# A cross-attention kernel's first context segment: from fp32 matmuls to three fp32r passes over split halves

## The chip, the cores and the metric

One Trainium2 chip, one of its cores. The metric is the device time of one execution in microseconds (us); the median of several runs is given. The engines of the core are PE (TensorE, the matrix engine), DVE (VectorE), ACT (ScalarE), POOL (GpSimd) and SP (SyncE, which issues the DMAs here). PEld stands for the weight loads of PE.

## What is computed

For 128 batches of 128 positions, x has 320 channels and the context 512. The context's 128 tokens fall into four segments: 77, 4, 4 and 43 tokens, each with weights of its own for keys and values. Attention runs with 20 heads of 16 channels; the four results are added.

```python
q = _heads(hidden_states @ to_q_w)
h_txt = _sdpa(q, _heads(ehs_txt @ to_k_w), _heads(ehs_txt @ to_v_w))
h_obj = _sdpa(q, _heads(ehs_obj @ to_k_object_w), _heads(ehs_obj @ to_v_object_w))
h_oth = _sdpa(q, _heads(ehs_oth @ to_k_others_w), _heads(ehs_oth @ to_v_others_w))
h_ip = _sdpa(q, _heads(ehs_ip @ to_k_ip_w), _heads(ehs_ip @ to_v_ip_w))
out = _merge(h_txt) + _merge(h_obj) + _merge(h_oth) + _merge(h_ip)
out = out @ to_out_w + to_out_b + hidden_states
```

## The kernel before

Four batches make a **group**, and there are 32 groups. The main loop has one **turn** g per group, and a turn has ten **slots**; each engine has its own program of slots (`groups`, line 271), and semaphores tie them together.

Attention works in **octets**: eight (batch, head) pairs, ten octets a group. In slot n:

- PE makes the scores of octet n + 2 (`scores`), transposes the probabilities of octet n - 2 in two quarters of four heads (`transpose_p`, line 913) and, in some slots, multiplies with the values (`values`, line 926) and with the output weights (`project`, line 936). The results of these three go through two PSUM banks, the ring, which ACT or DVE empties in turn.
- DVE takes the maxima of octet n + 1 and subtracts them (`reduce_max`, `shift`), then sums the exponentials of octet n and inverts the sums (`sum_up`, line 718, `invert`, line 729).
- ACT makes the exponentials of octet n (line 580) and copies PE's results.
- POOL multiplies the probabilities of octet n - 1 by the inverses (`scale`, lines 491 and 494). PE's transposition of an octet waits for it.

Between these, PE projects for the groups ahead. The **jobs** of a turn stand in `SEQ`: ("q", 0..2) make the queries of group g + 2, ("kv", 0..2) keys (and the head of the values) of group g + 2, ("kv", 3..4) the values of group g + 1, ("v", 0..3) transpose them. Two PSUM banks alternate between jobs; a job waits until the job two before it has left its bank. `PIECES` puts them into slots, by hand: a "kv" job comes in two halves.

```python
PIECES = [(0, 0, ("kv", 3), 0), (0, 1, ("kv", 3), 1), (1, 0, ("kv", 4), 0), (2, 0, ("kv", 4), 1), (3, 0, ("q", 0), None),
          (3, 1, ("v", 0), None), (4, 1, ("q", 1), None), (5, 0, ("v", 1), None), (5, 1, ("q", 2), None),
          (6, 0, ("v", 2), None), (6, 1, ("kv", 0), 0), (7, 0, ("kv", 0), 1), (7, 1, ("v", 3), None),
          (8, 0, ("kv", 1), 0), (8, 1, ("kv", 1), 1), (9, 0, ("kv", 2), 0), (9, 1, ("kv", 2), 1)]
```

A "kv" job (`work`, line 821) multiplies 128 rows of weights with the group's context `c_in`: half 0 is the first segment (77 tokens of four batches, 308 columns), half 1 the last segment (43 tokens, 172 columns). Both are fp32, four chunks of 512 channels; the trace shows each fp32 matmul as two records, so eight records a half (line 837). The two small segments were projected for all groups at the start (`small_job`, line 804) and are added by one matmul with the identity (line 847).

A query job is done in fp32r instead: x is split into a high half (ACT, `x_high`, line 574) and a low half (POOL, `x_low`, line 480), the weights as well, and three passes high·high, high·low and low·high are summed in PSUM (line 863). The projection at the end does the same with 320 columns (line 936).

A query or key job is then split into three bf16 parts: ACT writes the first (`evacuate`, line 562) once the job is done, DVE subtracts it from PSUM (`subtract_part`, line 708), which frees the bank, and POOL makes the other two (`split`, lines 472 and 475). SP stores them to scratch and loads them back as stacks (`store_parts`, `load_pair`). A stack pair holds two batches of a group.

POOL's program of a slot is, in this order: `scale` of octet n - 1, the splits of the jobs that ended two slots ago, `oT_low` (line 523) in slots 0, 2, 5 and 7, `x_low` in slots 9, 0 and 1. So slot 5 splits ("q", 0), slot 6 ("q", 1), slot 7 ("q", 2), slot 9 ("kv", 0). ACT's program of a slot is the exponential, evacuations, copies of the ring, evacuations, the spreading of values (line 613), `x_high`.

Context: `load_c(g + 2)` is issued in turn g once PE has finished ("kv", 4), in slot 2.

Before the loop, groups 0 and 1 are projected in `EARLY_JOBS`, and all weights are loaded and split. SP's order there is lines 376 to 412. `pads_made` counts memsets on DVE (lines 743 to 749) for which PE's first matmul waits. The projections of the small tokens for groups 2 to 31 lie in `pT` and go to scratch in one store of 2400 KB (line 406).

Of the kernel before, what the change touches and what calls it, by code (L numbers as in the profile page):

```python
# [5 lines left out]
B, S, T = 128, 128, 128  # L6
C, CA = 320, 512
H = 20
# [31 lines left out]
N_CONSTS = 5  # L40
N_PADS = 6
# [100 lines left out]
def xattn_kernel(nc: bass.Bass, x, xT, cT, cT_small, wq, wk, wv, wko, wvo, wkt, wvt, wki, wvi, wo, bo, out):  # L142
# [13 lines left out]
    with ExitStack() as stack:  # L156
# [12 lines left out]
        c_in = sb("c_in", [P, CK, NB, T])  # L169
        c_small = sb("c_small", [P, len(SMALL), CK, NB * B])  # L170
        x_res = sb("x_res", [P, 2, C])
# [3 lines left out]
        w_q2 = sb("w_q2", [P, 3, CT])  # L175
        w_kv = sb("w_kv", [P, len(LARGE), CK, 2 * C])
        w_q = [sb(f"w_q{i}", [P, 3, 3 * P], fp32r) for i in range(2)]
        w_o = [sb(f"w_o{i}", [P, 3, C], fp32r) for i in range(2)]
# [28 lines left out]
        wo_raw = y_all[:, 0:3 * C].rearrange("p (k c) -> p k c", k=3)  # L207
        v_flat = v_pad[:, :, :, :].rearrange("p b h w -> p (b h w)")

        s_ps = [banks(f"s_ps{i}", 2) for i in range(2)]  # L210
# [15 lines left out]
        x_lo_made = sem("x_lo_made")  # L226
        w_hi_made = sem("w_hi_made")
        w_lo_made = sem("w_lo_made")
        small_filled = sem("small_filled")
# [70 lines left out]

        W_FIRST = [(wq_raw[:, 0:2, :], w_q[0][:, 0:2, 0:C]), (wq_raw[P - CT:P, 2, :], w_q[0][P - CT:P, 2, 0:C]),
                   (wq_raw[0:CT, 2, :], w_q[1][0:CT, 2, 0:C])]
        W_SECOND = [(wq_raw[:, 0:2, :], w_q[0][:, 0:2, 0:C], w_q[1][:, 0:2, 0:C]),
                    (wq_raw[0:CT, 2, :], w_q[1][0:CT, 2, 0:C], w_q[0][0:CT, 2, 0:C])]

        @block.sync
        def _(sp):
# [63 lines left out]
            def load_w(dst, s, which, loaded):  # L371
                i = SMALL.index(s) if s in SMALL else LARGE.index(s)
                sp.dma_start(dst[:, i, :, which * C:(which + 1) * C],
                             seg_w[s][which].rearrange("(k p) c -> p k c", p=P)).then_inc(loaded, 16)
# [7 lines left out]
            for i in range(len(SMALL)):  # L382
                sp.dma_start(c_small[:, i, :, :], cT_small[i]).then_inc(few_loaded[i], 16)
                for which in range(2):
                    load_w(w_small, SMALL[i], which, few_loaded[i])
            load_c(0)
            for which in range(2):
                for s in LARGE:
                    load_w(w_kv, s, which, w_kv_loaded)
            load_x(1)  # L390
# [3 lines left out]
            sp.dma_start(wo_raw[0:CT, 2, :], wo[2 * P:C, :]).then_inc(w_o_loaded, 16)  # L394
            sp.wait_ge(pads_made, N_PADS)
            sp.dma_start(wo_raw[CT:CT + 1, 2, :], bo.rearrange("(a c) -> a c", a=1)).then_inc(w_o_loaded, 16)
# [54 lines left out]
        def _(pool):  # L451

            for t in w_q:
                pool.memset(t[:, :, C:3 * P].bitcast(fp32), 0.0).then_inc(consts_made, 1)
            pool.memset(zero[:, :], 0.0).then_inc(consts_made, 1)
# [20 lines left out]

            def x_low(g, k):
# [48 lines left out]
            def slot(g, n):  # L526

                if live(g * NO + n - 1, G * NO):
                    scale(g if n else g - 1, (n - 1) % NO)
                for at in range(2):  # L530
                    for turn, job in ended(g, n - 2, at):
                        if job in SPLITS:
                            split(turn + 2, SPLITS.index(job))
                if n in VALUES_AT and live(g * NB + VALUES_AT[n], B):
                    oT_low(g * NB + VALUES_AT[n])
                for k, (at, ahead) in enumerate(XLO_AT):
                    if at == n and live(g + ahead, G) and not (isinstance(g, int) and g + ahead < 3):
                        x_low(g + ahead, k)
# [4 lines left out]
        def _(act):  # L543
            def evacuate(turn, job):
# [12 lines left out]
                else:  # L557
# [57 lines left out]

            act.wait_ge(consts_made, 2)
            act.wait_ge(w_q_loaded, 16 * N_W_Q)
# [5 lines left out]
            act.wait_ge(consts_made, N_CONSTS)  # L623
            act.wait_ge(pads_made, N_PADS)
            for turn, job in EARLY_JOBS:
                evacuate(turn, job)
                if (turn, job) == (-2, ("q", 2)):
                    for k in range(CX):
                        x_high(1, k)
            spread(0, 0)  # L630
            spread(0, 1)
# [5 lines left out]
            def slot(g, n):  # L637
# [16 lines left out]
                if n in SPREAD_AT:  # L654
                    ahead, i = SPREAD_AT[n]
                    if live(g + ahead, G):
                        spread(g + ahead, i)
                for k, (at, ahead) in enumerate(XHI_AT):
                    if at == n and live(g + ahead, G) and not (isinstance(g, int) and g + ahead < 3):
# [5 lines left out]
        def _(dve):  # L665
# [81 lines left out]
            dve.memset(v_flat, 0.0).then_inc(pads_made, 1)  # L747
            dve.wait_ge(pads_made, N_PADS - 1)
            dve.memset(oT_raw[CT:CT + 1, 2, :], 1.0).then_inc(pads_made, 1)
# [8 lines left out]
            for turn, job in EARLY_JOBS:  # L758
# [3 lines left out]
                if (turn, job) == (-1, ("kv", 3)):  # L762
                    for n in range(len(SMALL) * MK, N_SMALL):
                        copy_small(n)
                if (turn, job) == EARLY_JOBS[-1]:
                    reduce_max(0, 0)
# [27 lines left out]
        def _(pe):  # L794

            def small_job(n):
# [6 lines left out]
                for k in range(CK):  # L803
                    last = pe.matmul(ring_ps[n % 2][:, :], w_small[:, i, k, m * P:(m + 1) * P], c_small[:, i, k, :],  # L804
                                     start=(k == 0), stop=(k == CK - 1))
# [15 lines left out]
            def work(turn, job, half=None):  # L821
# [56 lines left out]
            def scores(g, o):  # L878

                n = g * NO + o  # L880
                if o % NR == 0:
                    pe.wait_ge(stack_loaded[o // NR], (g + 1) * 16 * 2)
# [56 lines left out]

            pe.wait_ge(w_lo_made, len(W_SECOND))  # L940
            pe.wait_ge(pads_made, N_PADS)
            pe.wait_ge(ident_made, 1)
# [74 lines left out]
```

## Time and profile before

| | |
|---|---|
| median of 3 runs | 1705.54 us (1705.48 to 1706.51) |
| the profiled execution's own time | 1707.59 us |
| its span, first to last instruction | 1705.5 us |
| mean granted clock of TensorE | 0.992 of 2.4 GHz |
| PE, DVE, ACT, POOL busy | 95%, 88%, 63%, 79% |
| DMA | 366 MB, 215 GB/s |

Busy shares are of the span. A PE that is busy by its records is not PE at its peak, since matmuls overlap; where the pace of matmuls matters, the distance from start to start is read. Idle time in a row is that of the engine just before the instruction, with what released it.

### The profile page before, as it was taken

The numbers are of one execution on the slowest core, as the hardware profiler recorded it, in microseconds if no ns is written. First come the engines' busy times: TensorE is split into PE (matmuls) and PEld (weight loads), VectorE is DVE, ScalarE is ACT, GpSimd is POOL, SyncE is SP. The second block draws the span as 40 slices with busy tenths as digits, with TensorE's granted clock in tenths as the row PEclk, the third lists the DMA queues.
The fourth block names the chain that finished last, engine by engine and source line by source line (L and its number), as shares of the span: only waits on it lengthen the run. The fifth ranks groups of instructions, "written<-read, shape, count | busy, mean of one in ns | idle before, by whom it ended". The sixth has DMA issues, their size and how long they took to land.

```text
span 1705.5 us, 49968 instructions
## 1 busy us (share of the span) xinstructions
PE 1623.6 (95%) x15632; PEld 1377.6 (81%) x15632; DVE 1498.3 (88%) x3537; ACT 1076.2 (63%) x1989; POOL 1342.3 (79%) x1581
## 2 busy tenths in 40 slices
PE   6959999999999999999999999999999999999976
PEld 3658888888888888888888888888888888888865
DVE  4249999999999999999999999999999999999996
ACT  1126666666666666676666667666666666666664
POOL 4248888888888888888888888888888888888765
PEclk9979999999999999999999999999999999999999
DMA  8579889888988988898898889889888988988851
GB/s 303 140 208 234 205 228 239 203 227 217 241 206 227 237 205 227 217 238 209 227 235 205 227 218 238 208 230 232 207 226 219 238 208 231 230 207 229 207 124 32
DMA packets 423236, 366.24 MB, mean 215 GB/s; under 512 B 19041, under 2 KB 394274, under 8 KB 418850
## 3 DMA queue, kind: packets, MB, share of 16 engines
q1 hardware_dynamic: 423202, 365.80, 84.7%
q8 instruction: 20, 0.33, 0.1%
q14 instruction: 14, 0.11, 0.0%
HBM read 216.38 MB, written 149.34 MB: 214 GB/s over the span
## 4 chain that ended last, share of the span: by engine, by line
PE 71%; DVE 17%; issue 7%; POOL 2%; SPq 1%; DMA 1%; DVEq 1%; ACT 0%; POOLq 0%
PE job_ps L837 24%; PE ring_ps L913 13%; PE ring_ps L926 7%; PE ring_ps L936 7%; PE s_ps L886 6%; PE job_ps L863 5%; DVE l_seg L718 5%; DVE probs L691 5%; DVE m_seg L675 3%; PE job_ps L856 2%; PE ring_ps L804 2%; PE job_ps L866 2%; DVE rest L708 1%; POOL probs L491 1%; PE job_ps L874 1%
## 5 line engine op out<-in xcount | busy, mean ns | idle before, releaser
L491 POOL TENSOR_TENSOR probs<-probs,rl 128x616 f32<-128x616 f32 (+1 forms) x640 | 630.1, 1007 | 237.2 <-DVE rl L729 236.8
L837 PE MATMUL job_ps<-c_in,w_kv 128*128 128x172 f32 (+1 forms) x2560 | 575.5, 368 | 22.4 <-DVE rest L708 22.4
L592 ACT ACTIVATE pT<-ring_ps 128x512 f32<-128x512 f32 x640 | 378.6, 599 | 313.1 <-PE ring_ps L913 309.1
L837 PEld LDWEIGHTS job_ps<-c_in,w_kv 128*128 128x128 f32 x2560 | 421.4, 190 | 101.0 <-DVE rest L708 30.0
L718 DVE TENSOR_REDUCE l_seg<-probs 128x8 f32<-128x616 f32 (+1 forms) x640 | 385.4, 644 | 23.0 <-ACT probs L580 23.0
L913 PE MATMUL ring_ps<-ident,probs 128*128 128x128 f32 x2560 | 389.9, 277 | 10.1 <-DVE y_all L740 8.5
L691 DVE TENSOR_TENSOR probs<-s_ps,m_seg 128x616 f32<-128x616 f32 (+1 forms) x640 | 387.8, 648 | 0.0
L675 DVE TENSOR_REDUCE m_seg<-s_ps 128x8 f32<-128x616 f32 (+1 forms) x640 | 371.6, 623 | 3.5 <-issue 0.2
L580 ACT ACTIVATE probs<-probs 128x1024 f32<-128x1024 f32 x320 | 337.6, 1055 | 33.2 <-DVE probs L695 33.1
L913 PEld LDWEIGHTS ring_ps<-ident,probs 128*128 128x128 f32 x2560 | 290.0, 143 | 66.7 <-issue 25.1
L472 POOL TENSOR_TENSOR parts<-rest,zero 128x512 bf16<-128x512 f32 (+1 forms) x192 | 186.2, 970 | 50.7 <-DVE rest L708 50.7
L475 POOL TENSOR_TENSOR parts<-rest,parts 128x512 bf16<-128x512 f32 (+1 forms) x192 | 207.2, 1079 | 15.0
L708 DVE TENSOR_TENSOR rest<-job_ps,parts 128x512 f32<-128x512 f32 (+1 forms) x192 | 122.9, 640 | 109.4 <-ACT parts L562 109.3
L886 PE MATMUL s_ps<-k_all,q_all 128*128 128x128 bf16 x2560 | 197.6, 220 | 19.6 <-DVE probs L695 19.5
L936 PE MATMUL ring_ps<-w_o,oT 128*128 128x320 f32 x1152 | 202.1, 320 | 8.1 <-ACT pT L592 5.7
L886 PEld LDWEIGHTS s_ps<-k_all,q_all 128*128 128x128 bf16 x2560 | 163.8, 101 | 52.9 <-issue 24.7
L926 PE MATMUL ring_ps<-pT,v_pad 128*32 128x128 f32 x5120 | 194.7, 277 | 0.0
L936 PEld LDWEIGHTS ring_ps<-w_o,oT 128*128 128x128 f32 x1152 | 171.1, 189 | 15.1 <-ACT pT L592 12.5
L926 PEld LDWEIGHTS ring_ps<-pT,v_pad 128*32 128x32 f32 x5120 | 159.8, 110 | 14.0 <-issue 0.8
L599 ACT ACTIVATE oT_raw<-ring_ps 128x256 f32<-128x256 f32 x128 | 49.5, 387 | 172.3 <-PE ring_ps L926 171.6
L523 POOL TENSOR_TENSOR oT<-oT_raw,oT 128x384 fp32r<-128x384 f32 x128 | 128.4, 1003 | 27.8 <-ACT oT L605 27.8
L562 ACT ACTIVATE parts<-job_ps 128x512 bf16<-128x512 f32 (+1 forms) x192 | 106.6, 555 | 55.5 <-PE job_ps L847 37.0
(54 smaller groups left out, 1598.2 us busy)
## 6 DMA issues: line engine op xcount, KB each, us to landing
q_all<-q_scratch SPq DMA_DIRECT2D x64, 960.0 KB, 8.1
k_all<-k_scratch SPq DMA_DIRECT2D x64, 960.0 KB, 12.3
c_in<-in_cT SPq DMA_DIRECT2D x32, 1024.0 KB, 5.1
x_raw<-in_xT SPq DMA_DIRECT2D x32, 768.0 KB, 4.8
q_scratch<-parts SPq DMA_DIRECT2D x64, 384.0 KB, 3.0
k_scratch<-parts SPq DMA_DIRECT2D x64, 384.0 KB, 5.2
x_res<-in_x SPq DMA_DIRECT2D x128, 160.0 KB, 3.8
out<-y_all SPq DMA_DIRECT2D x128, 160.0 KB, 3.5
```

The source lines that it names most:

```text
L475: pool.tensor_tensor(dst[:, 2, :], src, dst[:, 1, :], ALU.subtract).then_inc(part3_made, 1)
L491: pool.tensor_tensor(pr[:, :, a:e], pr[:, :, a:e], r[:, :, s:s + 1].broadcast_to((P, OH, e - a)), ALU.mult)
L580: act.activation(pr, pr, ACT.Exp, scale=SCALE).then_inc(exp_done, 1)
L592: act.activation(pT[:, h:h + QH, :], ring_ps[i][:, :].rearrange("p (h s) -> p h s", h=QH), ACT.Copy)\
L675: dve.tensor_reduce(m_seg[:, o % 2, :, k:k + 1], sc[:, :, a:e], axis=AX.X, op=ALU.max)\
L691: dve.tensor_tensor(pr[:, :, a:e], sc[:, :, a:e], m_seg[:, o % 2, :, k:k + 1].broadcast_to((P, OH, e - a)), ALU.subtract)
L718: dve.tensor_reduce(l_seg[:, o % 2, :, s:s + 1], pr[:, :, a:e], axis=AX.X, op=ALU.add)
L837: last = pe.matmul(dst[:, :, a:e], w_kv[:, l, k, i * P:(i + 1) * P], c_in[:, k, :, a:e], start=(k == 0), stop=(k == CK - 1))
L886: last = pe.matmul(s_ps[o % 2][:, i * T:(i + 1) * T], q_st[s // 2][:, h, s % 2, :], k_st[s // 2][:, h, s % 2, :], start=True, stop=True)
L913: last = pe.transpose(ring_ps[i][:, k * S:(k + 1) * S], probs[:, (o % NR) * OH + q * QH + k, :], ident[:, :])
L926: last = pe.matmul(ring_ps[i][a * VW:(a + 1) * VW, k * S:(k + 1) * S], v_pad[:, s, h, :], pT[:, (s % 2) * H + h, :], start=(e == 0), stop= ...
L936: last = pe.matmul(ring_ps[i][:, 0:C], oT[a][:, k, :], w_o[c][:, k, :], start=(k == 0 and (a, c) == (0, 0)), stop=(k == 2 and (a, c) == (1 ...
```

## The change

The first segment's projection becomes three fp32r passes, as the queries' already are. Its width is rounded up to an even `W0` = 78 tokens, 312 columns for four batches (the column too many is overwritten by the matmul of the small tokens). The context's high halves `c0[0]` are made by ACT and the low halves `c0[1]` by POOL, in two pieces of two chunks each, 128x624: on ACT both at the end of slot 5, on POOL one each in slots 5 and 6, behind what these slots do already. The halves of a "kv" job are exchanged: half 0 is now the last segment (fp32, 172 columns), half 1 the first segment in 12 passes and the small tokens. The first of these passes for ("kv", 0) waits for both low halves. Group 0 keeps the fp32 matmuls.

The weights' halves `w0` take the room of `c_small` and part of `w_q`; so the small tokens' inputs are loaded into the second half of the stacks' memory, the raw weights into that of the padded values, and their memsets come later (`stacks_padded`, the last of `pads_made`). The unused zero columns of `w_q` fall away with their memsets on POOL. The 2400 KB store of the small tokens is issued before `load_c(1)`, no longer after three stores of group 1's queries, and the load of the second stack pair waits for the small jobs.

```diff
+W0 = SEGS[0][1] + SEGS[0][1] % 2
+CHI_AT, CLO_AT = [5, 5], [5, 6]
...
+        c_small = [t[:, H * 2 * S:NPAIR * H * 2 * S].bitcast(fp32)[:, 0:CK * NB * B].rearrange("p (k n) -> p k n", k=CK)
+                   for t in (q_all, k_all)]
...
             load_small(1)
+            sp.dma_start(small_scr[2:G].rearrange("g p n -> p g n"),
+                         small_all[:, 2:G, :, :, :].rearrange("p g m b t -> p g (m b t)")).then_inc(small_rest_stored, 16)
             load_c(1)
             for n in range(3):
                 store_parts(1, n)
-            sp.dma_start(small_scr[2:G].rearrange("g p n -> p g n"),
-                         small_all[:, 2:G, :, :, :].rearrange("p g m b t -> p g (m b t)")).then_inc(small_rest_stored, 16)
+            sp.wait_ge(small_filled, N_SMALL)
             load_pair(0, 0, 1)
...
+            def c_low(g, i):
+
+                pool.wait_ge(c_hi_made, (g - 1) * 2 + i + 1)
+                a = 2 * i
+                pool.tensor_tensor(c0[1][:, a:a + 2, :, :].rearrange("p k b t -> p (k b) t"),
+                                   c_in[:, a:a + 2, :, 0:W0].rearrange("p k b t -> p (k b) t"),
+                                   c0[0][:, a:a + 2, :, :].bitcast(fp32).rearrange("p k b t -> p (k b) t"), ALU.subtract)\
+                    .then_inc(c_lo_made, 1)
...
+            for m in range(MKV):
+                pool.wait_ge(w0_hi_made, m + 1)
+                pool.tensor_tensor(w0[1][:, :, m * P:(m + 1) * P], w0_raw[:, :, m * P:(m + 1) * P],
+                                   w0[0][:, :, m * P:(m + 1) * P].bitcast(fp32), ALU.subtract).then_inc(w0_lo_made, 1)
             for n in range(NSP):
+                if n == 3:
+                    for i in range(2):
+                        c_low(1, i)
                 split(1, n)
...
                     oT_low(g * NB + VALUES_AT[n])
+                for i in range(2):
+                    if CLO_AT[i] == n and live(g + 2, G):
+                        c_low(g + 2, i)
...
+            def c_high(g, i):
+
+                act.wait_ge(c_loaded, (g + 1) * 16)
+                act.activation(c0[0][:, 2 * i:2 * i + 2, :, :], c_in[:, 2 * i:2 * i + 2, :, 0:W0], ACT.Copy).then_inc(c_hi_made, 1)
...
                         spread(g + ahead, i)
+                for i in range(2):
+                    if CHI_AT[i] == n and live(g + 2, G):
+                        c_high(g + 2, i)
...
-            dve.memset(k_all[KS:P, :].bitcast(fp32), 0.0).then_inc(pads_made, 1)
-            dve.memset(q_all[KS:P, :].bitcast(fp32), 0.0).then_inc(pads_made, 1)
+            dve.memset(k_all[KS:P, 0:H * 2 * S].bitcast(fp32), 0.0).then_inc(pads_made, 1)
+            dve.memset(q_all[KS:P, 0:H * 2 * S].bitcast(fp32), 0.0).then_inc(pads_made, 1)
...
-                    for l, s in enumerate(LARGE):
-                        if half in (None, l):
-                            a, e = SEGS[s]
-                            for k in range(CK):
-                                last = pe.matmul(dst[:, :, a:e], w_kv[:, l, k, i * P:(i + 1) * P], c_in[:, k, :, a:e],
-                                                 start=(k == 0), stop=(k == CK - 1))
+                    if half in (None, 0):
+                        a, e = SEGS[3]
+                        for k in range(CK):
+                            pe.matmul(dst[:, :, a:e], w3[:, k, m], c_in[:, k, :, a:e], start=(k == 0), stop=(k == CK - 1))
...
+                    if half in (None, 1) and not whole_first:
+                        if i == 0:
+                            pe.wait_ge(c_lo_made, g * 2)
+                            if first:
+                                pe.wait_ge(w0_lo_made, MKV)
+                        for k in range(CK):
+                            for a, c in ((0, 0), (0, 1), (1, 0)):
+                                pe.matmul(dst[:, :, 0:W0], w0[a][:, k, m], c0[c][:, k, :, :],
+                                          start=(k == 0 and (a, c) == (0, 0)), stop=(k == CK - 1 and (a, c) == (1, 0)))
```

## Rows read from the trace of the kernel before

**Rows 1.** The page: busy time by engine; the chain that ended last, by engine.

```profile
PE 1623.6 (95%) x15632; PEld 1377.6 (81%) x15632; DVE 1498.3 (88%) x3537; ACT 1076.2 (63%) x1989; POOL 1342.3 (79%) x1581
...
PE 71%; DVE 17%; issue 7%; POOL 2%; SPq 1%; DMA 1%; DVEq 1%; ACT 0%; POOLq 0%
```

**Rows 2.** Timeline of PE: start us, us, instructions, [idle before <- releaser].

```profile
500.27 2.34 PE L837 MATMUL job_ps<-c_in,w_kv 128*128 128x308 f32 x8 [0.70 <-DVE rest L708]
...
823.85 0.63 PE L913 MATMUL ring_ps<-ident,probs 128*128 128x128 f32 x4
...
845.01 1.33 PE L837 MATMUL job_ps<-c_in,w_kv 128*128 128x172 f32 x8
...
846.32 0.64 PE L913 MATMUL ring_ps<-ident,probs 128*128 128x128 f32 x4
...
848.87 2.34 PE L837 MATMUL job_ps<-c_in,w_kv 128*128 128x308 f32 x8 [0.70 <-DVE rest L708]
```

**Rows 3.** Timeline of DVE, 800 to 852 us.

```profile
805.15 0.69 DVE L708 TENSOR_TENSOR rest<-job_ps,parts 128x512 f32<-128x512 f32 x1 [1.44 <-ACT parts L562]
...
826.59 1.21 DVE L718 TENSOR_REDUCE l_seg<-probs 128x8 f32<-128x616 f32 x2 [0.26 <-ACT probs L580]
...
848.14 0.68 DVE L708 TENSOR_TENSOR rest<-job_ps,parts 128x512 f32<-128x512 f32 x1
```

**Rows 4.** Chain that ended last, 800 to 840 us: start us, us.

```profile
801.85 1.33 PE ring_ps L936 x9
...
805.38 2.08 PE job_ps L837 x8
...
825.38 1.39 PE job_ps L863 x6
```

**Rows 5.** Timeline of ACT, slot 6's exponential.

```profile
836.89 1.07 ACT L580 ACTIVATE probs<-probs 128x1024 f32<-128x1024 f32 x1
```

**Rows 6.** Groups by line and shape: count | busy us, mean ns | idle before.

```profile
L480 POOL TENSOR_TENSOR x_lo<-x_raw,x_hi 128x512 fp32r<-128x512 f32 x96 | 122.3, 1276 | 20.3 <-ACT x_hi L574 20.2
...
L574 ACT ACTIVATE x_hi<-x_raw 128x512 fp32r<-128x512 f32 x96 | 56.1, 622 | 23.5 <-DMA x_raw<-in_xT 23.5
...
L501 POOL TENSOR_TENSOR w_q<-parts,w_q 128x640 fp32r<-128x640 f32 x1 | 1.5, 1544 | 5.9 <-ACT w_q L619 5.9
```

**Rows 7.** Timeline of POOL, slots 5 and 6 of a turn.

```profile
833.49 1.97 POOL L491 TENSOR_TENSOR probs<-probs,rl 128x616 f32<-128x616 f32 x2 [2.85 <-DVE rl L729]
...
835.68 1.04 POOL L472 TENSOR_TENSOR parts<-rest,zero 128x512 bf16<-128x512 f32 x1
...
837.91 1.01 POOL L523 TENSOR_TENSOR oT<-oT_raw,oT 128x384 fp32r<-128x384 f32 x1
838.88 1.98 POOL L491 TENSOR_TENSOR probs<-probs,rl 128x616 f32<-128x616 f32 x2
```

**Rows 8.** Timeline of SP's DMA issues, start-up.

```profile
90.09 0.59 SPq L406 DMA_DIRECT2D small_scratch<-pT  x1
...
106.17 0.43 SPq L330 DMA_DIRECT2D x_raw<-in_xT  x1
```

**Rows 9.** Timeline of ACT, start-up.

```profile
113.99 1.67 ACT L574 ACTIVATE x_hi<-x_raw 128x512 fp32r<-128x512 f32 x3 [14.25 <-DMA x_raw<-in_xT]
```

**Rows 10.** DMA issues: count, size, median us from issue to landing.

```profile
small_scratch<-pT SPq DMA_DIRECT2D x1, 2400.0 KB, 10.5
```

**Rows 11.** Busy time by stretch: length, engines, then PEclk, DMA share, GB/s.

```profile
75.00:90.00 15.00, 11.31 (x62) 8.30 (x62) 2.50 (x4) 4.20 (x9) 6.00 (x7) 1.00 0.63 201
100.00:105.00 5.00, 4.69 (x21) 3.76 (x22) 2.77 (x8) 0.00 (x0) 1.25 (x2) 0.68 1.16 221
```

**Rows 12.** Waits: engine, line <- releaser: us in total, times, longest us.

```profile
POOL parts L472 <- DVE rest L708: 50.7, 11, 20.3
```

**Rows 13.** Timeline of PE, start-up.

```profile
100.31 1.03 PE L886 MATMUL s_ps<-k_all,q_all 128*128 128x128 bf16 x8 [2.66 <-DVE probs L695]
101.14 4.47 PE L837 MATMUL job_ps<-c_in,w_kv 128*128 128x308 f32 x16
```

More of the change, by code:

```diff
@@ L39 @@
 N_SMALL = len(SMALL) * MKV
-N_CONSTS = 5
+N_CONSTS = 3
 N_PADS = 6
@@ L169, in xattn_kernel @@
         c_in = sb("c_in", [P, CK, NB, T])
-        c_small = sb("c_small", [P, len(SMALL), CK, NB * B])
+        c0 = [sb(f"c0_{i}", [P, CK, NB, W0], fp32r) for i in range(2)]
         x_res = sb("x_res", [P, 2, C])
@@ L175, in xattn_kernel @@
         w_q2 = sb("w_q2", [P, 3, CT])
-        w_kv = sb("w_kv", [P, len(LARGE), CK, 2 * C])
-        w_q = [sb(f"w_q{i}", [P, 3, 3 * P], fp32r) for i in range(2)]
+        w3 = sb("w3", [P, CK, 2 * C])
+        w0 = [sb(f"w0_{i}", [P, CK, 2 * C], fp32r) for i in range(2)]
+        w_q = [sb(f"w_q{i}", [P, 3, 2 * P], fp32r) for i in range(2)]
         w_o = [sb(f"w_o{i}", [P, 3, C], fp32r) for i in range(2)]
@@ L227, in xattn_kernel @@
         w_hi_made = sem("w_hi_made")
+        w0_hi_made = sem("w0_hi_made")
+        w0_lo_made = sem("w0_lo_made")
+        c_hi_made = sem("c_hi_made")
+        c_lo_made = sem("c_lo_made")
+        stacks_padded = sem("stacks_padded")
         w_lo_made = sem("w_lo_made")
@@ L382, in _ @@
             for i in range(len(SMALL)):
-                sp.dma_start(c_small[:, i, :, :], cT_small[i]).then_inc(few_loaded[i], 16)
+                sp.dma_start(c_small[i], cT_small[i]).then_inc(few_loaded[i], 16)
                 for which in range(2):
-                    load_w(w_small, SMALL[i], which, few_loaded[i])
+                    load_w(w_small[:, i, :, :], SMALL[i], which, few_loaded[i])
             load_c(0)
@@ L388, in _ @@
                 for s in LARGE:
-                    load_w(w_kv, s, which, w_kv_loaded)
+                    load_w(w0_raw if s == 0 else w3, s, which, w_kv_loaded)
             load_x(1)
@@ L623, in _ @@
             act.wait_ge(consts_made, N_CONSTS)
-            act.wait_ge(pads_made, N_PADS)
+            act.wait_ge(pads_made, N_PADS - 1)
             for turn, job in EARLY_JOBS:
+                if (turn, job) == (-1, ("kv", 0)):
+                    for i in range(2):
+                        c_high(1, i)
                 evacuate(turn, job)
@@ L629, in _ @@
                         x_high(1, k)
+                if (turn, job) == (-2, ("kv", 2)):
+                    act.wait_ge(w_kv_loaded, 16 * 4)
+                    for m in range(MKV):
+                        act.activation(w0[0][:, :, m * P:(m + 1) * P], w0_raw[:, :, m * P:(m + 1) * P], ACT.Copy)\
+                           .then_inc(w0_hi_made, 1)
+            act.wait_ge(pads_made, N_PADS)
             spread(0, 0)
@@ L657, in slot @@
                         spread(g + ahead, i)
+                for i in range(2):
+                    if CHI_AT[i] == n and live(g + 2, G):
+                        c_high(g + 2, i)
                 for k, (at, ahead) in enumerate(XHI_AT):
@@ L764, in _ @@
                         copy_small(n)
+                if (turn, job) == (-1, ("kv", 3)):
+                    for t in (k_all, q_all):
+                        dve.memset(t[KS:P, H * 2 * S:NPAIR * H * 2 * S].bitcast(fp32), 0.0).then_inc(stacks_padded, 1)
+                if (turn, job) == (-1, ("q", 1)):
+                    dve.wait_ge(w0_lo_made, MKV)
+                    dve.wait_ge(job_filled, job_count(-1, ("kv", MKV - 1)))
+                    dve.memset(v_flat, 0.0).then_inc(pads_made, 1)
                 if (turn, job) == EARLY_JOBS[-1]:
@@ L803, in small_job @@
                 for k in range(CK):
-                    last = pe.matmul(ring_ps[n % 2][:, :], w_small[:, i, k, m * P:(m + 1) * P], c_small[:, i, k, :],
+                    last = pe.matmul(ring_ps[n % 2][:, :], w_small[:, i, k, m * P:(m + 1) * P], c_small[i][:, k, :],
                                      start=(k == 0), stop=(k == CK - 1))
@@ L832, in work @@
                         pe.wait_ge(c_loaded, (g + 1) * 16)
-                    for l, s in enumerate(LARGE):
-                        if half in (None, l):
-                            a, e = SEGS[s]
-                            for k in range(CK):
-                                last = pe.matmul(dst[:, :, a:e], w_kv[:, l, k, i * P:(i + 1) * P], c_in[:, k, :, a:e],
-                                                 start=(k == 0), stop=(k == CK - 1))
+                    m = slice(i * P, (i + 1) * P)
+                    whole_first = isinstance(g, int) and g == 0
+                    if half in (None, 0):
+                        a, e = SEGS[3]
+                        for k in range(CK):
+                            pe.matmul(dst[:, :, a:e], w3[:, k, m], c_in[:, k, :, a:e], start=(k == 0), stop=(k == CK - 1))
+                    if half in (None, 1) and whole_first:
+                        a, e = SEGS[0]
+                        for k in range(CK):
+                            pe.matmul(dst[:, :, a:e], w0_raw[:, k, m], c_in[:, k, :, a:e], start=(k == 0),
+                                      stop=(k == CK - 1))
+                    if half in (None, 1) and not whole_first:
[3 more added lines that the diff above has]
+                                pe.wait_ge(w0_lo_made, MKV)
+                        for k in range(CK):
+                            for a, c in ((0, 0), (0, 1), (1, 0)):
+                                pe.matmul(dst[:, :, 0:W0], w0[a][:, k, m], c0[c][:, k, :, :],
+                                          start=(k == 0 and (a, c) == (0, 0)), stop=(k == CK - 1 and (a, c) == (1, 0)))
                     if half in (None, 1):
@@ L880, in scores @@
                 n = g * NO + o
+                if isinstance(g, int) and (g, o) == (0, NR):
+                    pe.wait_ge(stacks_padded, 2)
                 if o % NR == 0:
```

22 lines of the change are left out of this document (9 added, 13 removed).

## The prediction

> **What bounds the kernel now.** The page comes first: PE is busy 95% of the span, DVE 88%, and the chain that ended last is PE for 71% and DVE for 17% [rows 1]. So PE sets most of the time, but not all of it; the question is where in a turn of the loop DVE takes over. The PE timeline shows the period: the first half of ("kv", 1) starts at 500.27 and, seven turns later, at 848.87, so a turn is 49.80 us, and both times PE has idled 0.70 us for DVE's subtraction [rows 2]. It is the only idle time of PE in a steady turn.
>
> The DVE timeline says why [rows 3]. At 826.59 DVE begins a sum after an idle 0.26 us for ACT's exponential; from there to the subtraction of ("kv", 0) at 848.14 it has no idle time. So a turn has two legs. **Leg A**, PE-bound: from ("kv", 1) at 799.07 (848.87 less a turn) through ("kv", 2), 3 and 4 to the transposition at 823.85 [rows 2], then ACT, then DVE's sum at 826.59 [rows 3]: 27.52 us. DVE itself idled 1.44 us in it at 805.15 and 0.26 at its end, so it could end 1.70 us sooner if PE did. **Leg B**, DVE-bound: 826.59 to 848.87, 22.28 us.
>
> **What the passes save.** The first segment's half job is 8 records of 2.08 us in the chain; the fp32r projection does 9 passes over 320 columns in 1.33, 0.148 each, and 6 over 512 take 1.39, 0.232 each [rows 4]. Between them a column costs 0.44 ns, so 312 columns (four sequences of 78) take 0.1445 and 12 passes 1.73 us. The new shape is not in the trace: 0.145 and 0.232 are its ends, and I take the first, since 320 columns are nearest. A job saves 0.35 us. Leg A holds four such jobs: **-1.38 us**, less than DVE's 1.70, so all of it counts.
>
> **What the halves cost, in leg B.** A group gets two ACT copies and two POOL subtractions of 128x624.
> ACT: 512 elements take 0.622 us and 1024 take 1.07 [rows 5, 6], so 624 are about 0.72. They come at the end of slot 5, where the next thing on ACT is the exponential at 836.89 [rows 5], with the evacuation of ("q", 2) and the copy of a transposition behind it. All are pushed back by about 1.2 us; PE then waits for its ring about 1 us before ("kv", 0). That wait is covered: PE waits for POOL right after.
> POOL: the subtraction of 512 elements takes 1.276, of 640 1.544 [rows 6]; 624 are 1.51, and 1.47 from start to start. POOL waits 2.85 us for DVE, begins slot 5's scaling at 833.49, then the split of ("q", 0) at 835.68, the low half of oT at 837.91, the scaling at 838.88 [rows 7] and the split of ("q", 1). The new order, in the same frame: first low half 838.88 to 840.35, scaling (2.19, as from 833.49 to 835.68) to 842.54, split of ("q", 1) (2.23, from 835.68 to 837.91) to 844.77, second low half to 846.28.
> PE: the second half of ("kv", 0) began at 845.01 and the job ended at 846.32 [rows 2]. Now it is this half which needs both low halves. PE is there at about 845.1 (0.92 sooner, since the halves of a job are exchanged: 2.08 less 1.16, the 172 columns' share of it; and 1.0 later by the ring), and waits until 846.33. Then 1.73, 0.15 for the small tokens (1.31 from 845.01 to 846.32, less 1.16) and 0.1 added for the start after a wait: 848.31. **Behind the waiting matmuls** on PE stand the transposition at 846.32 [rows 2] and everything after it; ACT copies that transposition before it evacuates the job, and DVE subtracts 1.82 us after the job's end (846.32 to 848.14, [rows 2, 3]): now 850.13, with DVE waiting 1.99 us. PE's next ("kv", 1) needs that bank: 850.86 for 848.87. Leg B is **+1.99 us**.
> DVE's reciprocal needs POOL's scaling of two octets before; that one (842.54 at the latest) is still in time. The rest of POOL's 3 us falls into its waits for DVE.
>
> **A turn: -1.38 + 1.99 = +0.6 us; 30 turns have ("kv", 0): +18 us.** The drain after the last projections is DVE's and keeps its length.
>
> **The start-up.** SP issues the 2400 KB store of the small tokens at 90.09, ahead of the stack loads; x of group 2 is issued at 106.17 [rows 8], and ACT waits 14.25 us for it, until 113.99, before the first exponential can go [rows 9]. The change issues that store before the load of c(1), some 15 us sooner. It takes 10.5 us from issue to landing [rows 10]; the DMA engines were busy 0.63 of 75 to 90 us [rows 11], so 5.5 us of work fit there. Bounds 0 and 10.5; I take **-7 us**, near the 5.5, as the rest pushes c(1) and the stores of q back. c(1) then lands some 5 us late and the jobs of group 1 wait for its halves, which still ends before x of group 2 has landed. The halves of the first segment's weights (5 ACT copies, 5 POOL subtractions of about 1.3) lie in POOL's wait of up to 20.3 us [rows 12], the memsets put off in DVE's waits of the same stretch, the shorter memsets and query weights before the first matmul are ahead of this same landing: all nothing. Were the weights' cover gone, it would be 6.4 us once.
>
> **Sum.** The profiled execution took 1707.6 (span 1705.5 and 2.1 around it): 1707.6 + 18 - 7 = 1718.6. The median of the runs is 2.1 below the profiled time, so **1716.5**. Some 0.2% (3.4 us) is what a measurement can tell from no change.
>
> **Rivals.**
> - *The halves come in time (faster).* Place: PE's wait before the second half of ("kv", 0). If POOL had the second low half ready by about 844.4, leg B would not grow: 30 x -1.38 - 7 = -48, 1657. It decides at 1.9 us less on POOL than I count; break-even is a growth of leg B of 1.38 + 7/30 = 1.6. For it: POOL idles 2.85 us just before [rows 7]; if DVE's reciprocal came sooner, all would move. Against: that start is DVE's, and DVE is full. Chance 0.24, mostly of part of it, down to 1690.
> - *The two nearly cancel*, leg B growing by 1.5 to 1.7: 1702 to 1709. 0.15.
> - *The clock falls too.* After an idle 2.66 us at 100.31 [rows 13], PE's granted clock averaged 0.68 over 100 to 105 [rows 11], a mix of 1.2 and 2.4 GHz; the 16 records of a job at 101.14 took 4.47 [rows 13], against 2.08 + 1.16 in a turn. The new waits (1.2 and 0.9 us) are shorter than that one, though longer than 0.70. If each turn lost 1.1 us so: +33, about 1750. 0.04.
> - *The passes are no faster* (the change does not do what it says): at 0.232 each, 12 take 2.78. Leg A +2.8, leg B 1.99 + 1.05: 5.8 a turn, +175, about 1873. Against: nine projections at 0.148 [rows 4]. 0.02.
>
> The Trainium skill, in "TensorE: Matmul & The Clock Gate", section "The mechanism", says that a weight load overlaps with a running matmul only where the row groups differ; with its section "LDWEIGHTS" (128 columns at 1.2 GHz) a pass would by estimate be 107 + 130 = 237 ns and the sum that of the last rival. The projection's 148 ns [rows 4] contradict it, and the measurement decides.
>
> **How the numbers follow.** The forecast (slower) has 0.55. Its own range is 1703 to 1730: 0.02 us a pass is 0.24 us a job, so some 1 us in a turn, but so large an error is unlikely; 0.1 us on each POOL subtraction is 6 us in all, the start-up 5. For 8 in 10 I go from 1694 to 1738: it takes in the cancelling case and the mild part of the first rival. Faster 0.24, within 0.2% 0.15, slower 0.55 + 0.04 + 0.02 = 0.61.
>
> **What would show it.** Right: a PE idle of over 1 us each turn before the second half of ("kv", 0), released by POOL; a turn of about 50.4 us; x of group 2 landing 7 us sooner. Wrong: that half starting without a wait, a turn under 49.5 us; POOL's subtraction well off 1.5 us; passes off 0.145; ACT, through the delayed copies, appearing as PE's releaser instead of POOL.

## The result, and the profile after

**1708.68 us** in the median of 17 runs (1707.29 to 1711.47), beside 1706.26 (1705.26 to 1708.14) for the kernel before in as many runs on the same chips: a ratio of **1.0016**, 95% interval 1.0008 to 1.0023 (the two medians by themselves differ by 2.4 us, 0.14%). The change is a loss of 0.16%, smaller than the 0.6% forecast, and within the 0.2% that the prediction called the same. The profiled execution took 1708.46, of which 1706.7 are its span, 1.2 more than before.

The page of the kernel after, the lines that answer to [rows 1]:

```profile
PE 1582.3 (93%) x16252; PEld 1421.6 (83%) x16252; DVE 1497.4 (88%) x3539; ACT 1116.5 (65%) x2056; POOL 1431.4 (84%) x1646
...
POOL 60%; issue 25%; PE 7%; DVE 4%; POOLq 1%; DMA 1%; SPq 1%; ACT 1%; ACTq 0%
```

PE does 41 us less work than before, and the time does not follow. POOL does 89 us more, and the chain that ended last, which was PE for 71%, is now POOL for 60%. The question of the view is which POOL instruction PE waits for, and where in a turn. PE's timeline from slot 5 of one turn into slot 8, with ("kv", 1) of the next turn, the answer to [rows 2] (start us, us, instructions, idle before and its releaser):

```profile
835.80 1.58 PE L1003 MATMUL ring_ps<-w_o,oT 128*128 128x320 f32 x9 [0.87 <-ACT pT L626]
...
840.36 0.66 PE L980 MATMUL ring_ps<-ident,probs 128*128 128x128 f32 x4
841.91 2.00 PE L902 MATMUL job_ps<-c,w 128*128 128x312 f32 x12 [0.90 <-POOL c L491]
...
846.43 1.43 PE L889 MATMUL job_ps<-c_in,w 128*128 128x172 f32 x8 [0.68 <-DVE rest L753]
...
849.46 1.88 PE L902 MATMUL job_ps<-c,w 128*128 128x312 f32 x12
851.18 0.30 PE L912 MATMUL job_ps<-small,ident 128*128 128x32 f32 x2
...
896.56 1.43 PE L889 MATMUL job_ps<-c_in,w 128*128 128x172 f32 x8 [0.68 <-DVE rest L753]
```

A turn had one idle stretch of PE, 0.70 for DVE; now it has three: 0.87 for ACT at the ring, 0.90 for POOL's second low half ahead of the passes of ("kv", 0), and 0.68 for DVE ahead of ("kv", 1). ("kv", 1) starts at 846.43, and at 896.56 in the next turn: 50.13 us (50.14 in the mean of 29 turns), where it was 49.80. The twelve passes with no wait ahead of them run from 849.46 to 851.18, 1.72 in all.

The waits view says how often (total us, times, longest):

```profile
PE ring_ps L1003 <- ACT pT L626: 31.9, 37, 1.3
PE job_ps L902 <- POOL c L491: 27.6, 31, 0.9
PE job_ps L889 <- DVE rest L753: 21.2, 31, 0.7
```

POOL's timeline over the same slots, the answer to [rows 7]:

```profile
834.67 1.40 POOL L491 TENSOR_TENSOR c<-c_in,c 128x624 fp32r<-128x624 f32 x1
836.03 1.97 POOL L510 TENSOR_TENSOR probs<-probs,rl 128x616 f32<-128x616 f32 x2
...
838.23 1.04 POOL L482 TENSOR_TENSOR parts<-rest,zero 128x512 bf16<-128x512 f32 x1
...
840.46 1.40 POOL L491 TENSOR_TENSOR c<-c_in,c 128x624 fp32r<-128x624 f32 x1
```

Between the first subtraction's end and the second's start POOL is never idle: it makes the scaling and the split that its order puts there. The second ends at 841.86, and PE's half starts at 841.91. DVE's timeline gives the ends of the two legs, as in [rows 3]:

```profile
822.39 1.22 DVE L763 TENSOR_REDUCE l_seg<-probs 128x8 f32<-128x616 f32 x2 [0.62 <-ACT probs L614]
...
845.68 0.69 DVE L753 TENSOR_TENSOR rest<-job_ps,parts 128x512 f32<-128x512 f32 x1 [1.38 <-ACT parts L591]
```

Leg A runs from 796.29 (846.43 less 50.14) to 822.39: 26.10, which is **1.42 less** than before. Leg B, to 846.43, is 24.04: **1.76 more**. Over 30 turns the difference, 0.34 each, is 10.2 us; the span grew by 1.2 only, since the start-up gave back 9.0 in these two executions: x of group 2 is split at 104.97 instead of 113.99 [rows 9]. By the medians, which differ by 2.4, it gave back 7.8.

```profile
104.97 1.67 ACT L608 ACTIVATE x_hi<-x_raw 128x512 fp32r<-128x512 f32 x3 [0.59 <-DMA x_raw<-in_xT]
```

The prices of the halves, in the groups by shape (count | busy us, mean ns | idle before):

```profile
L491 POOL TENSOR_TENSOR c<-c_in,c 128x624 fp32r<-128x624 f32 x62 | 86.6, 1398 | 3.3 <-ACT c L600 3.3
...
L600 ACT ACTIVATE c<-c_in 128x624 fp32r<-128x624 f32 x62 | 41.7, 733 | 3.9 <-DMA c_in<-in_cT 3.9
```

### The profile page after: what moved, and what is told of

It reads as the page before. It is cut to its first block, busy times and chain, and to the rows that moved or that the text cites. A ratio compares the mean times of both kernels' runs of the same rounds, so it can differ in the third digit from the quotient of the medians.

```text
span 1706.7 us, 51429 instructions
## 1 busy us (share of the span) xinstructions
PE 1582.3 (93%) x16252; PEld 1421.6 (83%) x16252; DVE 1497.4 (88%) x3539; ACT 1116.5 (65%) x2056; POOL 1431.4 (84%) x1646
## 4 chain that ended last, share of the span: by engine, by line
POOL 60%; issue 25%; PE 7%; DVE 4%; POOLq 1%; DMA 1%; SPq 1%; ACT 1%; ACTq 0%
POOL probs L510 26%; POOL parts L482 9%; POOL x_lo L499 7%; POOL c L491 5%; POOL oT L549 5%; POOL probs L513 5%; POOL parts L485 3%; PE ring_ps L855 2%; DVE l_seg L763 1%; PE job_ps L902 1%; PE job_ps L889 1%; DVE probs L736 1%; DVE m_seg L720 1%; PE job_ps L893 1%; PE ring_ps L980 1%
## 5 line engine op out<-in xcount | busy, mean ns | idle before, releaser
L902 PE MATMUL job_ps<-c,w 128*128 128x312 f32 x1860 | 306.5, 314 | 27.6 <-POOL c L491 27.6
L902 PEld LDWEIGHTS job_ps<-c,w 128*128 128x128 f32 x1860 | 273.1, 190 | 35.1 <-POOL c L491 35.1
L889 PE MATMUL job_ps<-c_in,w 128*128 128x172 f32 x1280 | 219.0, 314 | 25.6 <-DVE rest L753 21.2
L889 PEld LDWEIGHTS job_ps<-c_in,w 128*128 128x128 f32 x1280 | 191.4, 192 | 34.2 <-DVE rest L753 28.6
```

What stands on the lines that cost most here:

```text
L889: pe.matmul(dst[:, :, a:e], w3[:, k, m], c_in[:, k, :, a:e], start=(k == 0), stop=(k == CK - 1))
L902: pe.matmul(dst[:, :, 0:W0], w0[a][:, k, m], c0[c][:, k, :, :], start=(k == 0 and (a, c) == (0, 0)), stop=(k == CK - 1 and (a, c) == (1, 0)))
```

## The experiments

The theory under test: the passes save what they should; the halves take it back through two places in a turn, ACT's copies in slot 5 (the ring) and POOL's order in slots 5 and 6 (the second low half); and the start-up hides part of it. Each run is compared with runs of the kernel before on the same chip.

### The slots of the halves

The edit is one line, the slots in which ACT makes the two high halves and POOL the two low ones:

```diff
-CHI_AT, CLO_AT = [5, 5], [5, 6]
+CHI_AT, CLO_AT = [5, 5], [5, 5]
```

> Both low halves in POOL's slot 5, ahead of the scaling and the split of slot 6; ACT unchanged. Theory: PE no longer waits for POOL, but still 0.87 us for the ring that ACT's copies hold: a turn of 49.25 us, 1708.7 - 30 x 0.9 = about 1682. Rival A (POOL alone sets leg B): 1656. Rival B (ACT alone sets it): 1708, unchanged.

Measured 1673.61 (1673.09 to 1675.41), ratio 0.9804 (0.9788 to 0.9821). Nothing is left out, only the second low half comes ahead of slot 6's scaling and split. PE's timeline over two turns, those of its waits that are in every turn:

```profile
821.58 1.59 PE L1003 MATMUL ring_ps<-w_o,oT 128*128 128x320 f32 x9 [0.87 <-ACT pT L626]
...
831.03 1.43 PE L889 MATMUL job_ps<-c_in,w 128*128 128x172 f32 x8 [0.42 <-DVE rest L753]
...
880.00 1.43 PE L889 MATMUL job_ps<-c_in,w 128*128 128x172 f32 x8 [0.39 <-DVE rest L753]
```

The wait for POOL is gone, ACT's 0.87 at the ring stays, a turn is 48.97. So the place of the second low half in POOL's order alone costs 50.14 less 48.97, **1.17 us a turn** and 35 us in all (1708.68 less 1673.61). The time fell between the two expectations, nearer to the theory's: 8.4 below it, as the wait for DVE ahead of ("kv", 1) shrank too, from 0.68 to about 0.4.

```diff
-CHI_AT, CLO_AT = [5, 5], [5, 6]
+CHI_AT, CLO_AT = [4, 4], [4, 5]
```

> Both high halves at the end of ACT's slot 4, the low halves at the end of POOL's slots 4 and 5. Theory (the second half of ("kv", 0) waits for POOL, and ACT's copies hold PE's ring): both waits of PE, 0.87 and 0.90 us, are gone, leg B is 22.3 us again, leg A keeps its -1.4: a turn of 48.4 us instead of 50.15, so 1708.7 - 30 x 1.75 = about 1656. Rival (the passes save nothing that counts): no more than the leg B growth comes back and leg A is lost to another wait: 1690 or above.

Measured **1661.55** (1661.02 to 1663.98), ratio 0.9739 (0.9723 to 0.9756), 5.5 above the theory's figure and far from its rival's. This version is faster than both kernels. Its waits of PE, those that come in each turn:

```profile
PE ring_ps L980 <- DVE y_all L785: 22.5, 35, 2.2
PE job_ps L889 <- DVE rest L753: 21.5, 31, 1.1
```

Neither ACT's ring nor POOL's half is among them; a turn is 48.59. Between this and the run ahead lie 0.38 us a turn, and two things had moved, one half on ACT's side and one on POOL's. This separates them:

```diff
-CHI_AT, CLO_AT = [5, 5], [5, 6]
+CHI_AT, CLO_AT = [4, 4], [5, 5]
```

> The kernel after, with both ACT copies in slot 4 and both POOL subtractions in slot 5. It separates what was left between halves in slots 4, 4 and 4, 5 (turn 48.59, 1661.6) and in slots 5, 5 and 5, 5 (turn 48.97, 1673.6). Theory: the 0.38 us a turn are ACT's two copies in slot 5, which hold up the transposition's copy and PE's ring for 0.87; with them in slot 4 PE does not wait for the ring, turn 48.6, 1661 to 1663. Rival: they are POOL's second subtraction in slot 5, which pushes its scaling and so DVE and the ring later: turn 48.9 to 49.0, 1672 to 1675.

Measured 1662.59 (1661.16 to 1663.0), ratio 0.9739 (0.9723 to 0.9755). The theory holds: with POOL's two subtractions still in slot 5 and ACT's copies in slot 4, the turn is 48.56 (("kv", 1) at 824.78 and 873.34). ACT's copies in slot 5 cost the 0.4 us, 11 us in all; POOL's subtractions side by side cost nothing there, though the scaling behind them is late enough to show:

```profile
819.89 0.66 PE L980 MATMUL ring_ps<-ident,probs 128*128 128x128 f32 x4 [0.50 <-DVE y_all L785]
...
824.13 0.63 PE L980 MATMUL ring_ps<-ident,probs 128*128 128x128 f32 x4 [0.47 <-POOL probs L513]
```

The 0.47 stands where PE else waited for DVE ahead of ("kv", 1); that wait is gone from the rows, so it replaced one rather than added one.

The last of the four puts ACT's copies early and leaves POOL as the change has it:

```diff
-CHI_AT, CLO_AT = [5, 5], [5, 6]
+CHI_AT, CLO_AT = [4, 4], [5, 6]
```

> Only the high halves move, to ACT's slot 4. Theory: PE's wait for the ring (0.87 us) goes, but its wait for POOL's second low half grows by as much, to 1.8 us, since POOL's order is the same: 1708, within 4 us. Rival B (ACT's copies set leg B): 1682.

Measured 1738.0 (1737.65 to 1739.79), ratio 1.0185 (1.0168 to 1.0202): 30 us above the theory's figure and 56 above its rival's. PE's timeline at the same place of two turns:

```profile
802.46 0.66 PE L980 MATMUL ring_ps<-ident,probs 128*128 128x128 f32 x4 [0.49 <-DVE y_all L785]
804.41 2.00 PE L902 MATMUL job_ps<-c,w 128*128 128x312 f32 x12 [1.29 <-POOL c L491]
...
852.62 0.66 PE L980 MATMUL ring_ps<-ident,probs 128*128 128x128 f32 x4 [0.49 <-DVE y_all L785]
854.55 2.83 PE L902 MATMUL job_ps<-c,w 128*128 128x312 f32 x12 [1.28 <-POOL c L491]
```

And the windows of these two stretches, and of the second one's surroundings up to 855.0 and from 855.5 on (length, engines, then PEclk, DMA share, GB/s):

```profile
804.00:807.00 3.00, 2.59 (x20) 2.59 (x21) 2.46 (x7) 0.17 (x1) 3.00 (x5) 1.00 1.00 328
854.00:857.50 3.50, 2.95 (x15) 2.95 (x16) 2.62 (x7) 0.32 (x1) 3.42 (x6) 0.70 0.94 314
...
852.50:855.00 2.50, 1.10 (x7) 0.87 (x8) 2.50 (x7) 1.22 (x4) 2.50 (x3) 1.00 0.37 129
855.50:858.00 2.50, 2.50 (x13) 2.50 (x12) 1.15 (x3) 0.00 (x0) 2.42 (x6) 0.50 0.78 254
```

The waits are the same in both, 0.49 and 1.28 or 1.29, together the 1.8 expected. The granted clock is 1.00 in the one stretch and 0.70 in the other: there it falls, just after PE has gone on, from 2.4 GHz to its lower level of 1.2, and the twelve passes take 2.83 instead of 2.00. A turn without the fall is 50.13, as in the theory, and one with it 51.3 to 51.7; of 29 turns 20 fell, and the 29.9 us by which all 29 exceed 29 times 50.13 are the miss. So the theory of the waits stands: the ring wait that ACT's copies made lay under POOL's, and without it a turn is as long. What the theory missed is the clock: with the ring wait PE idles 0.87 and 0.90 with 5.2 us of matmuls between, without it 0.49 and 1.28 with 0.66 between. Which of these differences lets the clock fall, no run here shows.

### The passes and the halves by themselves

```diff
-                for i in range(2):
-                    if CLO_AT[i] == n and live(g + 2, G):
-                        c_low(g + 2, i)
...
-                        if i == 0:
-                            pe.wait_ge(c_lo_made, g * 2)
-                            if first:
-                                pe.wait_ge(w0_lo_made, MKV)
+                        if i == 0 and first:
+                            pe.wait_ge(c_lo_made, 2)
+                            pe.wait_ge(w0_lo_made, MKV)
```

and ACT's loop with `c_high` goes as POOL's does.

> Leaves out the halves of all groups after the second: their first segment is multiplied with group 1's halves, in the same 12 passes. Theory (what the halves cost is PE's two waits and nothing else): a turn as with both waits gone, 48.4 to 48.6 us, so 1657 to 1663. Rival (the load on ACT and POOL costs time beyond the waits): below 1650.

Measured 1662.15 (1661.1 to 1662.61), ratio 0.9736 (0.9719 to 0.9754), within the theory's range:

```profile
825.00 1.43 PE L883 MATMUL job_ps<-c_in,w 128*128 128x172 f32 x8 [0.68 <-DVE rest L747]
...
873.57 1.43 PE L883 MATMUL job_ps<-c_in,w 128*128 128x172 f32 x8 [0.68 <-DVE rest L747]
```

A turn is 48.57, that of the slot orders 4, 4 and 4, 5 and 4, 4 and 5, 5; so **in those the halves cost nothing**, and the passes are worth 49.80 less 48.57, 1.23 a turn or 37 us in 30 turns. The other 7 of the 44 us come ahead of the turns: x of group 2 is split at 106.39 in this run, 7.6 sooner than in the kernel before.

```diff
                         for k in range(CK):
-                            for a, c in ((0, 0), (0, 1), (1, 0)):
-                                pe.matmul(dst[:, :, 0:W0], w0[a][:, k, m], c0[c][:, k, :, :],
+                            pe.matmul(dst[:, :, a:e], w0[0][:, k, m].bitcast(fp32), c_in[:, k, :, a:e], start=(k == 0),
...
```

> Makes all halves, in slots 5, 5 and 5, 6, but multiplies the first segment in fp32 with the high weights alone, from the context itself, in 8 records, with no wait for the low halves. Theory (ACT's copies hold the ring by 0.87 us, POOL's wait is gone, nothing is saved in leg A): a turn of about 50.7 us, 1706.3 - 9 + 27 = about 1724. Rival (the halves cost time through POOL's wait alone): 49.8 us a turn, 1697.

Measured 1726.07 (1725.45 to 1727.62), ratio 1.0116 (1.0098 to 1.0134). PE's waits over a turn:

```profile
802.22 1.44 PE L889 MATMUL job_ps<-c_in,w 128*128 128x172 f32 x8 [0.69 <-DVE rest L753]
...
843.16 1.59 PE L1003 MATMUL ring_ps<-w_o,oT 128*128 128x320 f32 x9 [0.88 <-ACT pT L626]
...
852.98 1.43 PE L889 MATMUL job_ps<-c_in,w 128*128 128x172 f32 x8 [0.69 <-DVE rest L753]
```

PE's wait for the low halves stands ahead of the last "kv" job instead, where it costs nothing. So no instruction in slot 6 waits for POOL, and a turn is 50.76, 0.96 above 49.80: about the size of ACT's 0.88 at the ring, which nothing covers. In the kernel after POOL's wait covers it; so the two waits are not to be added up.

### The start-up

Two kernels move the 2400 KB store of the small tokens' projections, one back in the kernel after, one forward in the kernel before:

```diff
-            sp.dma_start(small_scr[2:G].rearrange("g p n -> p g n"),
-                         small_all[:, 2:G, :, :, :].rearrange("p g m b t -> p g (m b t)")).then_inc(small_rest_stored, 16)
             load_c(1)
             for n in range(3):
                 store_parts(1, n)
+            sp.dma_start(small_scr[2:G].rearrange("g p n -> p g n"),
+                         small_all[:, 2:G, :, :, :].rearrange("p g m b t -> p g (m b t)")).then_inc(small_rest_stored, 16)
```

> The 2400 KB store goes back behind the three stores of group 1's queries. Theory: x of group 2 lands 9 us later again and everything behind it moves by that: 1708.7 + 9 = about 1717.7. Rival (the start-up gain is the 2.4 us by which the first matmul is sooner, and the earlier weights): 1711 or less.

Measured 1713.45 (1713.18 to 1713.58), ratio 1.0039 (1.0025 to 1.0053): between the two. ACT's timeline shows the split of x of group 2, against 104.97 in the kernel after:

```profile
110.63 1.67 ACT L608 ACTIVATE x_hi<-x_raw 128x512 fp32r<-128x512 f32 x3 [11.25 <-DMA x_raw<-in_xT]
```

By this split the store's place gives 5.7 of the 9.0, by the times 4.8 (1713.45 less 1708.68). The reverse edit, in the kernel before:

> The kernel before with nothing but its 2400 KB store issued ahead of the load of c(1). Theory (the store's place is worth 5.7 us by itself): 1700.6. Rival (it needs the earlier first matmul): 1706, no change.

Measured 1701.02 (1699.0 to 1703.39, nine runs), ratio 0.9967 (0.9957 to 0.9978), as the theory had it, with the split 5.0 sooner:

```profile
108.96 1.67 ACT L574 ACTIVATE x_hi<-x_raw 128x512 fp32r<-128x512 f32 x3 [1.01 <-DMA x_raw<-in_xT]
```

A single split is not that exact. Up to it, six more of the kernels here (the four slot orders, the passes without the halves, and the one with more subtractions at POOL's end, below) are the same program as the kernel after, and they split x of group 2 between 103.70 and 106.68; these are the earliest and the latest, of the orders 4, 4 and 4, 5 and 4, 4 and 5, 5:

```profile
103.70 1.67 ACT L608 ACTIVATE x_hi<-x_raw 128x512 fp32r<-128x512 f32 x3 [0.86 <-DMA x_raw<-in_xT]
...
106.68 1.65 ACT L608 ACTIVATE x_hi<-x_raw 128x512 fp32r<-128x512 f32 x3
```

The mean of the seven is 105.6. The store's some 5 us are clear of that scatter; that the rest is just 3.3 is not. It was to be the first matmul's, at 13.08 in the kernel after and 15.46 in the one before:

```profile
13.08 0.76 PE L928 MATMUL job_ps<-x_hi,w_q 128*128 128x512 f32 x1 [13.08 <-POOL x_lo L499]
...
15.46 0.77 PE L863 MATMUL job_ps<-x_hi,w_q 128*128 128x512 f32 x1 [15.46 <-DVE oT_raw L749]
```

This edit holds it up:

```diff
+            again = sem("again")
+            dve.wait_ge(pads_made, 2)
+            for n in range(3):
+                dve.memset(k_all[KS:P, 0:H * 2 * S].bitcast(fp32), 0.0).then_inc(again, 1)
+                dve.wait_ge(again, n + 1)
             dve.memset(wo_raw[CT:P, 2, :], 0.0).then_inc(pads_made, 1)
```

> The kernel after, with three more memsets of the same stack rows on DVE ahead of the first matmul (3 x 2.7 us, from 2.19 each and 0.5 between two), so that DVE's start-up memsets end at about 15.2 us instead of 7.2, where those of the kernel before ended (15.4). Theory: of the 9.0 us by which x of group 2 came earlier, 5.7 were the store's place and the other 3.3 came from the first matmul at 13.08 instead of 15.46. Then the first matmul goes back to about 15.3, x of group 2 is split at 107.2 to 108.3 instead of 104.97, and the time is 1711 to 1712. Rival: the earlier first matmul is hidden ahead of the landing, as the prediction had it, and the 3.3 come from the DMA queue's order alone: the split stays within 0.5 of 104.97 and the time within 1 of 1708.7.

Measured 1711.67 (1710.94 to 1712.78), ratio 1.0030 (1.0020 to 1.0041): 3.0 above the kernel after, as the theory had it. ACT, and PE's first matmul, in this run, then SP's issue of x of group 2 in the kernel after and here:

```profile
108.05 1.67 ACT L608 ACTIVATE x_hi<-x_raw 128x512 fp32r<-128x512 f32 x3 [1.41 <-DMA x_raw<-in_xT]
...
15.70 0.77 PE L933 MATMUL job_ps<-x_hi,w_q 128*128 128x512 f32 x1 [15.70 <-DVE oT_raw L798]
...
97.17 0.43 SPq L341 DMA_DIRECT2D x_raw<-in_xT  x1
...
99.87 0.43 SPq L341 DMA_DIRECT2D x_raw<-in_xT  x1
```

The first matmul is 2.62 later than in the kernel after, SP issues x of group 2 2.70 later, and the split comes 3.08 later. Both lie outside what the seven kernels above show (issues from 95.85 to 98.20, mean 97.2) and are 2.6 and 2.5 behind their means. So what is late at the start arrives late at the end of the start-up, about one for one.

### The price of POOL's subtraction

The expected 1.51 was read from rows of 512 and 640 elements. Eighteen more subtractions stand after POOL's last work, on the same tiles:

```diff
+            for n, part in ((512, None), (624, None), (640, None), (624, 78), (640, 80), (616, 77), (312, 78), (1024, 128), (512, 64)):
+                for _ in range(2):
+                    d, src, l = three(n, part)
+                    pool.tensor_tensor(d, src, l, ALU.subtract).then_inc(shape_made, 1)
+                    count += 1
+                    pool.wait_ge(shape_made, count)
```

> Adds 18 subtractions to POOL's program behind its last work: fp32r results of 512, 624 and 640 elements in one row, and of 8x78, 8x80, 8x77, 4x78, 8x128 and 8x64, each twice. If the price goes by elements alone, 624 take 1.40 us in either form and 640 about 1.43, and the weights' 1.54 for 640 had another cause; if one long row is dearer than rows of 78, 624 in one row take about 1.5. The time itself is some 20 us longer.

The added line's instructions in four stretches: 624 and 640 elements in one row, then 624 as eight rows of 78 and 640 as eight of 80 (count: duration ns, least, median and most, then first and last start):

```profile
L588 POOL TENSOR_TENSOR c<-c_in,c x2: 1497/1497/1497, 1704.7 to 1706.3; 128x624 fp32r<-128x624 f32 x2
...
L588 POOL TENSOR_TENSOR c<-c_in,c x2: 1530/1531/1532, 1707.9 to 1709.5; 128x640 fp32r<-128x640 f32 x2
...
L588 POOL TENSOR_TENSOR c<-c_in,c x2: 1392/1394/1395, 1711.1 to 1712.6; 128x624 fp32r<-128x624 f32 x2
...
L588 POOL TENSOR_TENSOR c<-c_in,c x2: 1535/1536/1536, 1714.0 to 1715.7; 128x640 fp32r<-128x640 f32 x2
```

The same 624 elements take 1.497 in one row and 1.394 in rows of 78, the price of the kernel after (1.398), so for 624 the form of the rows decides and the elements alone do not; but 640 take 1.53 in either form. The interpolation of the prediction was right for one long row, and the change uses rows of 78. Why these are cheaper and rows of 80 are not stays open.

## Why the prediction came out as it did

**The direction and the mechanism were right**, step by step:

- *The passes*: forecast 0.1445 each, 1.73 for twelve; measured 1.72, so 0.143. Leg A: forecast 1.38 less, measured 1.42. The 1.70 of DVE's idle time that the forecast set beside it left out two more stretches in leg A, 0.88 at 811.10 and 0.42 at 820.48; as 1.38 was below it already, nothing hangs on that. The Trainium skill's sentence that a weight load overlaps with a running matmul only where the row groups differ ("TensorE: Matmul & The Clock Gate", section "The mechanism"), by which the forecast estimated 237 ns a pass, is contradicted by these passes, each with its own load, as it was by the projection's [rows 4]. The same section of the Trainium skill also lets a load into the background weight buffer go ahead of running matmuls; the forecast left that out, and no run here can tell whether it is what happened.
- *ACT's copies*: 0.72 forecast, 0.733 measured; the ring wait "about 1 us", measured 0.87, and covered by POOL's wait. Without that wait it costs 0.96 a turn (the run with the halves alone).
- *The wait that takes back the gain*: PE ahead of the second half of ("kv", 0), released by POOL, 1.2 forecast, 0.90 measured, 31 times. The sign "over 1 us" so did not come true: POOL was ready 0.22 sooner than forecast, for the reason below, and PE came 0.11 later. From the wait's end to ("kv", 1) it is 4.52, where the forecast had 4.53.
- *c(1) late*: forecast 5 us; PE waited 4.44 for c_in once, at 86.36.

**Two terms were mis-sized, both to the same side**, the first clear of the scatter.

- *POOL's subtraction, "624 are 1.51"*: 1.398. Counted from the sum of leg B, the second low half was to end 19.69 after it (826.59 to 846.28) and ended after 19.47 (822.39 to 841.86); the 0.22 are two subtractions at 0.11. Leg B therefore grew by 1.76 instead of 1.99, and the turn by 0.34 instead of 0.60: over 30 turns 7.8 us. Of these, 6.6 are POOL's price and the rest leg A's 0.04. The step that failed is the choice of price by element count; the row nearest by count was not the nearest by form.
- *The start-up, "-7" and "all nothing"*: measured -9.0 between the two profiled executions, -7.8 by the medians. The sum was nearly right, by two errors that offset each other. The store gave 4.8 to 5.9 instead of 7, close to the 5.5 of idle DMA time that the prediction worked out before it went up to 7. The "all nothing" was wrong: with the shorter memsets and query weights PE begins 2.4 us sooner, and the delayed run shows that such a start is worth some 2.5 to 3 us at the end. The prediction held that all this lies ahead of x's landing and is hidden by it; but x's issue on SP moves about one for one with the first matmul. The memsets and the smaller weights were not tried apart.

Between the profiled executions it is 7.8 + 2.0 = 9.8, and that is by how much the span came out below the forecast's (+1.2 instead of 18 - 7 = +11). Between the medians (+2.4) it is 7.8 and 0.8. So the turn, not the start-up, made the forecast's loss too large.

**The rivals.** *The two nearly cancel* had the time right (1702 to 1709), by other terms: leg B grew a little more than that case allowed, and the start-up gave 1 to 2 us more. That the time lay there is luck as far as the start-up goes. *The halves come in time* is the true alternative: it did not happen here, but with slots 4, 4 and 4, 5 it does, at 1661.6 instead of the 1657 worked out for it. *The clock falls too* did not come true in the kernel after: in all 29 turns the twelve passes behind the wait read 1.99 or 2.00. It did in the kernel with slots 4, 4 and 5, 6, in 20 of 29 turns, at 29.9/20 = 1.50 us for a turn that fell (1.1 was the estimate).

## What to carry to other kernels

Work taken off the bounding engine counts only up to the next wait in the same turn: here the passes were worth 37 us, and the place of one 1.4 us subtraction in POOL's order took 35. When operands are made by another engine, ask where in that engine's written order they stand and what lies ahead of them, and place them one slot ahead of the scarce stretch before judging the change. A forecast that is a small difference of two large terms needs each to a few per cent, so take a price from a row of the same form, and follow a start-up from issue to issue, in more than one execution: here the same start-up ended up to 3 us apart.

## What the runs showed of the hardware

- **The clock fell behind two short waits close together, and not behind two further apart.** In the kernel with slots 4, 4 and 5, 6, PE idled 0.49 and 1.28 us with one transposition of 0.66 between them, and in 20 of 29 turns the passes behind them took 2.6 us or more instead of 2.00 (a granted clock of 0.70 over the 3.5 us from 854.00). In the kernel after, 0.87 and 0.90 with 5.2 us of matmuls between them left the passes at 2.00 in every turn. Whether it is the pair or the longer single wait that decides, and why some of the turns with the same waits keep the clock, is open.
- **A subtraction on POOL is priced by its rows too**: 1.39 us for 8 rows of 78, 1.50 for one of 624, 1.53 to 1.54 for 640 in one row or 8 of 80.
